# Two edits to a macaron transformer layer: the up-weight loads move to ScalarE's DMA queue, and the first attention transposes wait for less

## The reference

```python
def _bitlinear(x, w):
    return jnp.einsum('bsi,oi->bso', _act_quant(x), _weight_quant(w))
gate = jax.nn.silu(_bitlinear(x, w_gate))
up = _bitlinear(x, w_up)
return _bitlinear(gate * up, w_down)
...
K = jnp.exp(_linear(x, Wk1, bk1))
K_cum = jnp.cumsum(K, axis=1) + 1e-06
S = jnp.cumsum(K * V, axis=1) / K_cum
Q = jax.nn.sigmoid(_linear(x, Wq1, bq1))
O_ar = S * Q
E = jnp.concatenate([zero, V[:, 1:, :] - O_ar[:, :-1, :]], axis=1)
K2 = _ma_k_activation(_linear(qk2_in, Wk2, bk2))
S2 = jnp.cumsum(K2 * E, axis=1)
Q2 = jnp.concatenate([zero, _ma_q_activation(Q)[:, :-1, :]], axis=1)
return _linear(O_ar + S2 * Q2, Wproj, bproj)
...
x = x + 0.5 * _L0_ffn_ref(_layernorm(x, axis=-1), w_gate, w_up, w_down)
x = x + _L0_attn_ref(_layernorm(x, axis=-1), ...)
x = x + 0.5 * _L0_ffn_ref(_layernorm(x, axis=-1), w_gate, w_up, w_down)
```

## Time and profile before

| what | us |
|---|---|
| median of the timed runs (2, 6755.49 to 6764.9) | 6760.19 |
| the profiled execution, slowest core | 6763.96 |
| its span, core 3 | 6762.7 |
| spans of the eight cores | 6689.4 to 6762.7 |
| TensorE matmuls busy | 3981.3 |
| VectorE busy | 2510.4 |
| ScalarE busy | 1721.8 |

### The profile page before, as it was taken

How to read it: one execution, slowest core, us unless ns; L and a number is a source line. 1 busy time by engine, 2 the same in 40 slices (tenths; PEclk the granted TensorE clock), 3 DMA queues, 4 the chain that set the end, 5 groups by cost and what they waited for, 6 DMA issues and landing times.

```text
span 6762.7 us, 57150 instructions; the slowest of 8 cores (6689.4 to 6762.7 us)
## 1 busy us (share of the span) xinstructions
PE 3981.3 (59%) x19026; PEld 2097.8 (31%) x19026; DVE 2510.4 (37%) x4103; ACT 1721.8 (25%) x2272; POOL 476.9 (7%) x505
## 2 busy tenths in 40 slices
PE   0007636774567647576367745676475763777457
PEld 0004413333233323334133332333233441333323
DVE  4543164123532253231641244322532316412352
ACT  4543113122131212231130221312122311312212
POOL 0000120002100020001200020000200012000200
PEclk6559868887889868788688877897687886888788
DMA  7993622425314333226224252143332252232532
GB/s 220 283 279 90 121 52 75 131 90 86 87 64 140 83 67 100 91 91 120 55 69 138 86 94 81 63 137 84 66 100 88 93 115 49 79 119 89 92 88 87
DMA packets 229228, 699.99 MB, mean 104 GB/s; under 512 B 22096, under 2 KB 22096, under 8 KB 224848
## 3 DMA queue, kind: packets, MB, share of 16 engines
q0 software_dynamic: 76576, 159.41, 13.1%
q1 hardware_dynamic: 78640, 268.47, 13.0%
q10 hardware_dynamic: 73728, 268.47, 12.5%
HBM read 788.55 MB, written 41.94 MB: 123 GB/s over the span
## 4 chain that ended last, share of the span: by engine, by line
PE 40%; DVE 21%; DMA 16%; ACT 14%; issue 7%; POOL 1%; DVEq 1%; ACTq 0%; SPq 0%; POOLq 0%
PE PB L621 11%; PE PB L626 11%; PE PB L703 9%; DMA sarena<-sc_d 8%; PE PB L773 5%; PE PB L421 4%; DVE pool L591 3%; ACT qi L454 2%; ACT pool L662 2%; ACT poolb L458 2%; DVE smal L597 1%; DMA poolb<-wq1t 1%; ACT pool L588 1%; ACT pool L789 1%; DMA pool<-wut 1%
## 5 line engine op out<-in xcount | busy, mean ns | idle before, releaser
L621 PE MATMUL PB<-sarena,poolb 128*128 128x512 bf16 x4096 | 1580.8, 386 | 433.5 <-DMA sarena<-sc_g 169.5
L626 PE MATMUL PB<-sarena,poolb 128*128 128x512 bf16 x4096 | 1579.9, 386 | 0.0
L703 PE MATMUL PB<-sarena,poolb 128*128 128x512 bf16 x4096 | 959.6, 392 | 208.3 <-DMA sarena<-sc_d 207.2
L421 PE MATMUL PB<-ident,pool 128*128 128x128 f32 x2144 | 482.4, 361 | 969.7 <-ACT pool L535 366.1
L591 DVE SCALAR_TENSOR_TENSOR pool<-PB,smal,pool 128x512 f32<-128x512 f32 x512 | 382.0, 746 | 1422.2 <-ACT pool L588 1422.2
L621 PEld LDWEIGHTS PB<-sarena,poolb 128*128 128x128 bf16 x4096 | 405.7, 99 | 997.4 <-issue 554.7
L588 ACT ACTIVATE pool<-PB,smal 128x512 f32<-128x512 f32 x512 | 326.7, 686 | 1414.8 <-PE PB L626 1383.6
L421 PEld LDWEIGHTS PB<-ident,pool 128*128 128x128 f32 x2144 | 367.7, 192 | 1009.8 <-issue 1008.1
L703 PEld LDWEIGHTS PB<-sarena,poolb 128*128 128x128 bf16 x4096 | 397.9, 100 | 766.0 <-issue 358.6
L626 PEld LDWEIGHTS PB<-sarena,poolb 128*128 128x128 bf16 x4096 | 405.5, 99 | 474.9 <-issue 31.1
L773 PE MATMUL PB<-poolb 128*128 128x256 bf16 x3072 | 405.3, 299 | 162.6 <-ACT pool L789 125.5
(11 more groups left out here) (141 smaller groups left out, 3230.1 us busy)
## 6 DMA issues: line engine op xcount, KB each, us to landing
sarena<-sc_u SPq DMA_DIRECT2D x256, 512.0 KB, 4.8
sarena<-sc_g ACTq DMA_DIRECT2D x256, 512.0 KB, 5.4
sarena<-sc_d ACTq DMA_DIRECT2D x256, 512.0 KB, 3.8
pool<-wgt SPq DMA_DIRECT2D x32, 1024.0 KB, 10.6
pool<-wut SPq DMA_DIRECT2D x32, 1024.0 KB, 10.9
pool<-wdt SPq DMA_DIRECT2D x32, 1024.0 KB, 10.8
poolb<-wk1t POOLq DMA_DIRECT2D x64, 512.0 KB, 7.8
poolb<-wq1t POOLq DMA_DIRECT2D x64, 512.0 KB, 7.8
```

Of the source, the lines that this page charges most:

```text
L421: TE.transpose(out=PB[:, b * 1024 + j * 128: b * 1024 + (j + 1) * 128], in_=s_, identity=ident[:, :])
L621: TE.matmul(out=pb[ttg * 4 + (tt % 2)][:, :], lhsT=aq[:, tt, ic, :], rhs=gsl[:, bsel * 2048 + ic4 * 512: bsel * 2048 + (ic4 + 1) * 512], s ...
L626: tl_ = TE.matmul(out=pb[ttg * 4 + 2 + (tt % 2)][:, :], lhsT=aq[:, tt, ic, :], rhs=usl[:, bsel * 2048 + ic4 * 512: bsel * 2048 + (ic4 + 1) ...
L703: tl_ = TE.matmul(out=pb[tt * 2 + obk][:, :], lhsT=hq[:, tt, ic, :], rhs=dsl[:, bsel * 2048 + ic2 * 1024 + obk * 512: bsel * 2048 + ic2 * ...
```

## The change

The load of the up weights in `gu_load` is issued by ScalarE, right behind the load of the gate weights, and the wait that SyncE had in front of it is gone with it. And the attention's first transposes take as their VectorE count the one reached when tiles 0 and 1 had been added to x (`dn_floor`), not the one reached after tiles 2 and 3; their ScalarE count stays as it was.

```diff
--- before.py
+++ after.py
@@ -458,6 +458,8 @@
                     cS.inc(S.add(out=dst, in_=qiS[:, 0:w_],
                                  add=nm128_ap))
 
+    dn_floor = [0]
+
     def xstage(tt):
         hs, ti = tt // 2, tt % 2
         return VT[:, :, hs * 256 + ti * 128:hs * 256 + ti * 128 + 128]
@@ -566,8 +568,7 @@
                             [[8 * 512, 128], [512, 4], [1, 512]])
             dGU[bs].inc(S.dma_start(
                 out=gsl[:, bs * 2048:(bs + 1) * 2048], in_=src_g), 16)
-            SY.wait_ge(cT.h, gu_arena_cT[bs])
-            dGU[bs].inc(SY.dma_start(
+            dGU[bs].inc(S.dma_start(
                 out=usl[:, bs * 2048:(bs + 1) * 2048], in_=src_u), 16)
 
         if c == 0:
@@ -719,6 +720,7 @@
                     in1=xb[:, tt, obk * 512:(obk + 1) * 512],
                     op0=ALU.mult, op1=ALU.add)
         cV.inc(vl_)
+        dn_floor[0] = cV.n
         if attn_next is not None:
             attn_next()
         cV.wait(V)
@@ -796,10 +798,11 @@
 
         def emit_half_mms(th):
             tt0 = th * 2
+            sv = (dn_floor[0], cS.n) if th == 0 else None
             transpose_quads(
                 [([xstage(tt)[:, dc, :] for dc in range(DC)],
                   xn2T[:, :, 1 + tt * 128:1 + (tt + 1) * 128])
-                 for tt in (tt0, tt0 + 1)])
+                 for tt in (tt0, tt0 + 1)], saved=sv)
             transpose_quads(
                 [([xb[:, tt, dc * 128:(dc + 1) * 128] for dc in range(DC)],
                   VT[:, :, tt * 128:(tt + 1) * 128])
```

## The result

| | before | changed |
|---|---|---|
| median of the timed runs, us | 6759.9 (6 runs) | 6689.6 (7 runs) |
| the profiled execution, us | 6763.96 | 6671.39 |
| its spans, slowest core, mean of the 8 cores, us | 6762.7, 6724.8 | 6670.3, 6650.4 |

The ratio of the changed kernel to the one before is 0.990, with a 95% interval of 0.989 to 0.992. The kernel became about 1% faster, 66 to 70 us, where the forecast was 103.

A forecast was written before the change was run, and what follows sets the result against it. Bound by TensorE, waiting at chunk boundaries for up loads queued behind the store of y and load of x. Terms 112.6 - 9 - 5 + 2 + 0 + 2.4 = 103 us gave 6657 us, range 6618 to 6705.

The forecast's parts named there:

- signs of being wrong: sc_u waits over more than some 20 of 256 steps; boundary gaps over 9 us; second FFN starts above 9 us.
- The boundary starts: Seven chunk boundaries: TensorE's idle time falls from 158.9 to 46.3 us, a gain of 112.6.
- a queue is served in order: Boundary loads: the first of two lands 0.8 us or more ahead of the second, hence the gain of 112.6 us.
- The other end of the term: Boundaries: four loads share the engines and land together, 8.5 us of idle each, a gain of 99.4 us.
- x beside TensorE's work: Step 2's load pair shares evenly with x, 1.5 us late at six boundaries: 9 us lost, ends 0 and 23.
- Steady steps: 224 later gate/up steps: pairs from one queue sometimes land late, 5 us lost, between 0 and 22.
- Rival (a): Every load pair: a queue serves one load only after the last has landed; 6939 us, 2.6% slower; chance 0.05.
- The second FFN's starts: Eight starts, u now following g: 0.3 us less each, 2 us gained; ends a loss of 15, a gain of 5.
- The second edit: First attention transposes: the wait ends 0.3 us earlier, 8 times, 2.4 us gained; ends 0 and 3.
- The clock: Matmuls after a boundary at 1.2 GHz: shorter idle might spare slow starts; taken as 0, ends 0 and 17 us.

The follow-up runs named there:

- experiment 3: Changed kernel, with ScalarE waiting at each FFN's head until slot 0's two loads have landed before issuing slot 1's: 6706.8 us, ratio 0.988.
- experiment 2: Changed kernel, with the load of the next x moved behind the gate and up steps of the chunk's first FFN: 6685.4 us, ratio 0.988.
- the first edit alone: Kernel before, with only the up loads moved to ScalarE and the attention transposes waiting as before: 6707.1 us, ratio 0.991.
- the second edit alone: Kernel before, with only the attention transposes' shorter wait and the up loads left on SyncE: 6762.1 us, ratio 0.999.
- experiment 5: Changed kernel with y and x later, and each later FFN's first two slots loaded after the previous FFN's gate and up steps: 6624.5 us, ratio 0.975.

## Why the prediction was right, and what it missed

The time lies in the range and has the right sign; the gain came out a third smaller than forecast, 65 to 74 us in the means of the cores' spans, 66 to 70 in the timed runs, against 103. The range, 87 us wide, left room for that; two terms turned out as losses where the forecast had a gain or nothing, and one came out right by luck. One of the prediction's own signs of being wrong is there: the second FFN starts average 9.5 us, above its 9.

*The boundary starts.* Forecast 158.9 to 46.3, measured 158.0 to 53.9 us, 104 of the 112.6. What was wrong is the sentence "a queue is served in order". u(0) as the second of four takes 6.5 us in the median of 42 boundary starts (5.4 to 9.3), where the second of two took 4.9 (4.6 to 6.7). Slot 1's loads, held back in experiment 3, are what delays it. The other end of the term, 8.5 us a start, was not reached either: 7.7.

*x beside TensorE's work.* Forecast 9 us for even sharing, measured 10.2, and experiment 2 shows that it is x and nothing else. But the size is right by luck. The working had the pair land after 7.9 us, 1.5 late; behind a load of x it took 10.0 in the median (36 cases), near the 10.3 of a pair that waits for all of x, and TensorE waited 3.7 us. Of these, 2.0 were not new: before the third step VectorE makes TensorE wait as long in the kernel before too, which the working left out. The Trainium skill, "DMA: Bandwidth & Descriptors", section on queues, rings and completion order, has the engines take turns between queues that hold work. The trace agrees in so far as both are slowed, the pair from 5.8 to 10.0 us and x from 8.3 to 11.3; it doesn't show that they share evenly.

*Steady steps.* Forecast 5, measured 2.7 us in this pair of profiles; the four other profiles with u on ScalarE and no other edit to the weight loads have 79 to 83 us of these waits, the four others with u on SyncE 73 to 76, so 5 is about right. Rival (a), that a queue serves one load after another has landed, is excluded: the u loads have a median of 5.5 us.

*The second FFN's starts.* Forecast a gain of 2, measured a loss of 6.6 us. This step failed in sign, for the reason of the first and because of when u leaves: u used to leave 2.3 us ahead of g on its own queue, and g then had little left to wait for; now four loads leave together behind ScalarE's last conversion. The prediction gave a loss of 15 as the end of this term.

*The second edit.* Forecast 2.4, measured 2 us.

*The clock.* Forecast 0, with 0 to 17 of gain as ends. This is the other term that failed: it is a loss, outside these ends. The slow matmuls right behind the starts stayed as they were (in the first 9 us behind 15 starts, 62.6 us at the lower level before and 64.8 after, half of it lost). But in the stretch 13 to 24 us behind a start the lower level, 1.2 GHz, shows up more often. Here are these stretches behind the first four second FFN starts from chunk 1 on, in the changed kernel (length, PE, PEld, DVE, ACT and POOL busy, granted clock, DMA share, GB/s):

```profile
1783.90:1794.90 11.00, 8.97 (x35) 3.57 (x33) 5.47 (x8) 3.93 (x5) 0.00 (x0) 0.84 0.41 136
2555.10:2566.10 11.00, 8.97 (x35) 3.58 (x34) 5.47 (x8) 3.93 (x5) 0.00 (x0) 0.84 0.50 134
3333.20:3344.20 11.00, 8.97 (x34) 3.58 (x33) 5.47 (x8) 3.93 (x5) 0.00 (x0) 0.84 0.39 142
4109.70:4120.70 11.00, 8.96 (x42) 3.94 (x41) 5.48 (x8) 3.63 (x5) 0.00 (x0) 1.00 0.33 114
```

and in the kernel before:

```profile
1794.50:1805.50 11.00, 8.97 (x42) 3.94 (x41) 5.47 (x8) 2.96 (x5) 0.00 (x0) 1.00 0.31 100
2578.70:2589.70 11.00, 8.97 (x42) 3.95 (x41) 5.47 (x8) 3.41 (x5) 0.00 (x0) 1.00 0.48 146
3364.00:3375.00 11.00, 8.97 (x43) 3.89 (x42) 5.47 (x8) 3.32 (x5) 0.00 (x0) 1.00 0.36 111
4153.60:4164.60 11.00, 8.96 (x35) 3.59 (x33) 5.47 (x8) 3.93 (x5) 0.00 (x0) 0.84 0.44 148
```

0.84 means that the clock was at 1.2 GHz for a third of the stretch, and TensorE then did 35 matmuls of the step instead of 42. Summed over 15 stages (all but the first; their first 9 us, this stretch and all later steps), a core spent 102.9 us at the lower level in the changed kernel and 82.5 before; half of the difference, 10 us, is lost time. Most of it is in this stretch of the second FFNs, 14.2 us against 4.6. In the other profiles the sum was 99.9 and 104.3 us for the first edit alone and for the changed kernel again, 73.1 for the second edit alone, and 72.4 for the kernel with y and x later and u on SyncE. In front of these stretches TensorE has waited 9 to 10 us at the start and 2 us in front of the third step. In the profiles of all runs this stretch goes with those starts: 14 to 17 us at the lower level in the five profiles whose second FFN starts sum to 76 or 77 us, 2 to 5 in the six with 67 to 70. That the longer waits bring the clock down was not tested by itself, and stays open.

The sum of the terms as measured: 104.1 - 10.2 - 2.7 - 6.6 + 2 - 10 = 77 us, against 65 in the spans of the same six cores. The difference of 12 is the +10.1 us of the table's fifth row and the 2 us that the transposes' gain hides in it: 2.3 us at the first start, the rest in the attention and down stages, which vary by as much between the two profiles of the changed kernel (1920 and 1910 us). No term of the prediction stands for it. The two cores left out gained 104 us, which makes the 74 of all eight.

## What to carry to other kernels

When a load is late, look at what its queue does before it: an instruction that waits for a store to land holds up every load behind it on that engine, and the cure is to get the load ahead of it. That can be done by moving the load, but moving the store and the next input to a stretch without other DMA traffic brought more here, because it also keeps them from meeting the loads that a stage needs on time. And loads that are not needed yet should not leave with those that are: four under way at once, on one queue or on two, delayed the two that were needed.

## What the runs showed of the hardware that was not expected

- Four 512 KB loads issued within 1.4 us on one queue are not served one after the other: the second landed after 6.5 us in the median (5.4 to 9.3, 42 boundary starts), against 4.9 (4.6 to 6.7) when only two were under way. From two queues the first pair of four took as long as from one, 6.9 and 6.8 us.
- After waits of 2.4 to 3.6 us in front of the second FFN (experiment 5) the first 9 us of matmuls ran at the full clock in 39 of 48 starts. Behind the waits of 6.6 us and more in the kernels before and after, all 180 starts had 2.6 to 6.0 us at 1.2 GHz, and so lost 1.3 to 3.0 us.
